# Transformer block on one core: queries projected transposed, with the two heads' halves sorted by transfers inside SBUF

## The reference

```python
mod = silu(c) @ wmod                      # per batch: sa, ca, ga, sb, cb, gb
h = layernorm(x) * (1 + ca) + sa
fused = h @ w_kv_a                        # q_c (192), kv_c (64), k_pe (64)
q = rmsnorm(q_c) @ w_qb                   # 16 heads of 128 (nope) + 64 (rotary)
kv = rmsnorm(kv_c) @ w_kvb                # per head: k_nope (128), v (128)
q_pe = q_pe * cos + rotate_half(q_pe) * sin     # and k_pe alike
scores = q_full . k_full / sqrt(192), causal softmax, @ v, @ w_o
x = x + ga * attention
h = layernorm(x) * (1 + cb) + sb
# 16 routed experts, top 4, at most 128 tokens each, and one shared expert
x = x + gb * (experts(h) + shared(h))
```

## Time and profile before

| what | value |
|---|---|
| median of 3 runs | 1230.08 us (1229.61 to 1230.75) |
| span of the profiled execution | 1228.7 us (its only own time on record) |
| TensorE / VectorE / ScalarE / POOL busy | 95% / 68% / 54% / 23% of the span |
| mean granted TensorE clock | 0.982 |
| first scores | 53.9 us |
| distance between pairs in mid-batch | 12.20 us |

### The profile page before, as it was taken

The page is one execution under the profiler, slowest core; times in us unless marked ns, Lnnn a source line. Parts: engine busy times, 40 slices in busy tenths (PEclk is TensorE's granted clock), DMA queues, the critical chain, the costliest instruction groups (busy, mean ns, idle before and its releaser), DMA issues.

```text
span 1228.7 us, 26041 instructions
## 1 busy us (share of the span) xinstructions
PE 1165.9 (95%) x7596; PEld 954.4 (78%) x7596; DVE 836.3 (68%) x2596; ACT 666.3 (54%) x1904; POOL 276.5 (23%) x332
## 2 busy tenths in 40 slices
PE   6799999999999999999999999999999999998792
PEld 3688878887788878887788779887788778886561
DVE  3577758776677668776777568776777668764541
ACT  2477635774477635774467626773467636672130
POOL 1000032221322132121312022211312122212364
PEclk8899999999999999999999999999999999999897
DMA  9520002000010001000010001000110001000793
GB/s 296 154 62 0 0 4 67 0 0 0 17 51 0 0 17 51 0 0 0 17 51 0 0 17 51 0 0 0 33 36 0 0 17 34 1 1 18 228 234 38
DMA packets 48157, 46.01 MB, mean 37 GB/s; under 512 B 10050, under 2 KB 44800, under 8 KB 48136
## 3 DMA queue, kind: packets, MB, share of 16 engines
q1 hardware_dynamic: 29096, 30.90, 8.5%
q0 software_dynamic: 7168, 6.20, 2.7%
q10 hardware_dynamic: 11872, 8.65, 2.5%
HBM read 35.04 MB, written 15.11 MB: 41 GB/s over the span
## 4 chain that ended last, share of the span: by engine, by line
PE 86%; DVE 4%; ACT 2%; POOL 2%; DMA 2%; SPq 1%; issue 1%; ACTq 1%; POOLq 0%; DVEq 0%
PE PS L691 11%; PE PS L712 11%; PE PS L830 8%; PE PS L670 7%; PE PS L671 6%; PE PS L672 6%; PE PS L656 4%; PE PS L838 4%; PE PS L859 3%; PE PS L643 3%; PE PS L646 3%; PE PS L647 3%; PE PS L644 2%; PE PS L645 2%; PE PS L809 2%; PE PS L701 2%
## 5 line engine op out<-in xcount | busy, mean ns | idle before, releaser
L1031 ACT ACTIVATE probs<-probs,nmax 128x512 f32<-128x512 f32 (+3 forms) x512 | 283.5, 555 | 167.6 <-DVE nmax L1275 164.1
L1275 DVE CUSTOM_DVE_ANT_0 probs<-PS,cmask 128x512 f32<-128x512 f32 (+3 forms) x512 | 230.4, 488 | 117.0 <-PE PS L672 114.7
L552 POOL DMA_INDIRECT tab_dram<-entry,slot x112 | 110.5, 987 | 386.7 <-PE PS L712 365.4
L670 PE MATMUL PS<-kTh,qTh 128*128 128x512 f32 (+3 forms) x512 | 174.5, 341 | 1.5 <-DVE qTl L1306 1.5
L672 PE MATMUL PS<-kTh,qTl 128*128 128x512 f32 (+3 forms) x512 | 164.9, 322 | 0.0
L671 PE MATMUL PS<-kTl,qTh 128*128 128x512 f32 (+3 forms) x512 | 164.9, 322 | 0.0
L691 PE MATMUL PS<-ident,probs 128*128 128x128 f32 x1280 | 164.8, 275 | 0.0
L1040 ACT ACTIVATE pT<-PS 128x384 f32<-128x384 f32 (+3 forms) x320 | 124.4, 461 | 68.0 <-PE PS L691 68.0
L712 PE MATMUL PS<-pT,kmat 128*64 128x512 f32 (+3 forms) x1024 | 151.9, 439 | 0.3 <-issue 0.3
L691 PEld LDWEIGHTS PS<-ident,probs 128*128 128x128 f32 x1280 | 141.4, 140 | 10.3 <-issue 7.4
L712 PEld LDWEIGHTS PS<-pT,kmat 128*64 128x64 f32 x1024 | 68.0, 136 | 76.0 <-issue 62.1
(11 more groups left out here) (256 smaller groups left out, 2084.8 us busy)
## 6 DMA issues: line engine op xcount, KB each, us to landing
x_in<-in_x SPq DMA_DIRECT2D x8, 512.0 KB, 6.0
modb<-mod_dram SPq DMA_DIRECT2D x8, 512.0 KB, 5.4
h_dram<-mod_dram SPq DMA_DIRECT2D x1, 4096.0 KB
h_dram<-h SPq DMA_DIRECT2D x8, 512.0 KB, 3.0
out<-base SPq DMA_DIRECT2D x8, 512.0 KB, 3.5
pT<-in_wo SPq DMA_DIRECT2D x1, 2048.0 KB, 11.0
tab_dram<-entry,slot POOLq DMA_INDIRECT x112, 2.1
oT<-in_wqnT SPq DMA_DIRECT2D x1, 1536.0 KB, 11.5
```

The source lines that it names most:

```text
L552: pool.indirect_dma_start(tab_dram[:, :], bass.IndirectOffsetOnAxis(ap=slot[:, j:j + 1], axis=0), entry[:, j, :], None, bounds_check=NE * ...
L670: pe.matmul(PS[:, bank, 0:n], qTh[:, h, rows_q], kTh[:, 0:n], start=True, stop=False)
L1031: act.activation(probs[:, UO[u]:UO[u] + UW[u]], probs[:, UO[u]:UO[u] + UW[u]], ACT.Exp, scale=-1.0, bias=nmax[:, u:u + 1], accum_out=psums ...
L1275: dve.tensor_tensor_reduce(out=probs[:, UO[u]:UO[u] + UW[u]], in0=PS[:, SBANK[u], 0:UW[u]], in1=cmask[:, S - UW[u]:S], scale=-1.0, scalar= ...
```

## The change

Queries are projected transposed: the weights (128 columns: latent or rotary numbers of both heads of a pair) are stationary and all 512 tokens move, so a pair's queries come out with features in rows, the latent ones in bank 6 and the rotary ones in bank 7. Rotation is done in this form, with tables by row: VectorE multiplies by cosine, and by sine for two 64-row halves crosswise; POOL adds, ScalarE makes the high part, POOL the low part. ScalarE and VectorE make the latent high and low part. All four lie in `qstage`, in which the rows are not sorted by heads; SP sorts them by six transfers inside SBUF into `qT` (two buffers), and the scores wait for these. This runs two pairs ahead instead of one. The pair loops are unrolled. In steps 6 and 7 outputs stand where the projections stood, and the h1 statistics and turns have moved to step 6.

```diff
+            def move(p, hl, lo, head, frm, n):
+                src = qstage[frm:frm + n, 2 * hl:2 * hl + 2, :].bitcast(F32)
+                sp.dma_start(qT[p % 2][lo:lo + n, :, head, :].bitcast(F32), src).then_inc(q_landed[p % 2], 16)
+            def move_query(b, p, fresh=False):
+                g = b * NPAIR + p
+                wait_alone(sp, latl_ready, g + 1)
+                if not fresh:
+                    wait_alone(sp, s_ps, NU * (g - 1))
+                for h in range(2):
+                    move(p, 0, 0, h, h * KL, KL)
+                wait_alone(sp, pel_ready, g + 1)
+                for h in range(2):
+                    for half in range(2):
+                        move(p, 1, KL + half * HALF, h, half * KL + h * HALF, HALF)
...
             sp.dma_start(h2_dram[0:T, H:].rearrange("(b s) h -> b s h", s=S),
                          mod_dram[:, 3 * H:].unsqueeze(1).to_broadcast([B, S, H])).then_inc(gates_out, 16)
+            for p in range(3):
+                move_query(0, p, p < 2)
             with sp.Fori(0, B - 1) as b:
                 n = b + 1
                 sp.wait_ge(h1_ready, n)
                 sp.wait_ge(res_ready, n)
                 sp.dma_start(x_in[:], rows(xr, n)).then_inc(x_landed, 16)
+                for p in range(3, NPAIR):
+                    move_query(b, p)
+                for p in range(2):
+                    move_query(n, p)
+                store_rows(b)
+                move_query(n, 2)
                 store_batch(b)
                 load_modb(n)
...
+            def query_rotary(g):
+                wait_alone(pool, turned_ready, g + 1)
+                pool.tensor_tensor(qr[:, 0, :], qr[:, 0, :], qr[:, 1, :], ALU.add).then_inc(rope_ready, 1)
+                wait_alone(pool, peh_ready, g + 1)
+                pool.tensor_tensor(qstage[:, 3, :], qr[:, 0, :], qstage[:, 2, :].bitcast(F32),
+                                   ALU.subtract).then_inc(pel_ready, 1)
...
+            with pool.Fori(0, B - 1) as b:
+                n = b + 1
+                roots_pre(n)
+                roots_post(b)
+                query_rotary(n * NPAIR)
+                rows_scaled(b)
+                query_rotary(n * NPAIR + 1)
+                rows_shifted(b, n)
+                counts(b, False)
+                query_rotary(n * NPAIR + 2)
+                shared(b)
+                for p in range(1, NPAIR - 1):
+                    if p + 2 < NPAIR:
+                        query_rotary(n * NPAIR + p + 2)
+                    scatter(b, p)
+                pool.wait_ge(scattered, n * NT * TOPK * 16)
                 pool.sem_inc(entries_free, 1)
...
-            def q_project(p, g, tiles):
-
-                cols = bass.ts(p, 2 * P)
...
+            def q_project(p, bank):
+
+                cols = bass.ts(2 * p + (bank == PEBANK), P)
+                pe.matmul(PS[:, bank, :], wq0h[:, cols], ql0h[:], start=True, stop=False)
...
+                    if u == 0:
+                        pe.wait_ge(q_landed[p % 2], landed(b, p))
...
+                last = p == NPAIR - 1
+                if p < NPAIR - 2:
+                    q_rotary(p + 2, g + 2)
+                elif not last:
+                    pe.wait_ge(turned_ready, (b + 1) * NPAIR)
                     pe.wait_ge(oT_ready, g)
-                    pe.wait_ge(qTl_ready, 2 * g + 2)
-                    output(1, 7, range(0, 3))
+                    output(1, PEBANK, range(0, 3))
                 else:
-                    q_project(p + 1, g + 1, (0, 1))
+                    if more:
+                        turn_h1(b + 1, 1, LATBANK)
+                    pe.wait_ge(oT_ready, g)
+                    output(1, PEBANK, (NPAIR - 3,))
...
+                scores(b, p, first, (3, 4))
+                if p < NPAIR - 2:
+                    q_latent(p + 2, g + 2)
+                elif not last:
+                    output(1, PEBANK, range(3, NPAIR - 3))
...
+                    output(0, LATBANK, range(0, 3))
+                scores(b, p, first, (5, 6, 7))
                 if not first:
                     values(g - 1, b)
...
                 turn_probs(g, first, (0, 1))
...
+                if last:
+                    output(0, LATBANK, range(3, NPAIR - 2))
                 turn_probs(g, first, (2, 3))
...
+                if p == NPAIR - 2 and more:
+                    pe.wait_ge(latl_ready, (b + 1) * NPAIR)
+                    turn_h1(b + 1, 0, LATBANK)
                 turn_probs(g, first, (4, 5))
                 spread_sums(g)
...
+                act.activation(qstage[:, 0, :], PS[:, LATBANK, :], ACT.Copy).then_inc(lath_ready, 1)
+
+            def rotary_high(b, p):
+                act.wait_ge(rope_ready, b * NPAIR + p + 1)
+                act.activation(qstage[:, 2, :], qr[:, 0, :], ACT.Copy).then_inc(peh_ready, 1)
...
                 maxima(g, (3, 4))
                 if first and more:
                     gated(b - 1, 0)
-                if last and more:
+                if p == NPAIR - 2 and more:
                     modulation(b + 1)
                     h1_statistics(b + 1)
+                for part in rope[:1]:
+                    part()
                 maxima(g, (5, 6, 7))
...
+                for part in rope[1:]:
+                    part()
+                if p == NPAIR - 2 and more:
                     h1_normed(b + 1)
                 invert_sums(g)
+                if rope and not first:
+                    q_low(g + 2)
```

More of the change, by code:

```diff
@@ L729, in step @@
                     shared_down(0)
-                scores(g, first, (3, 4))
-                if last:
-                    output(1, 7, range(3, NPAIR - 2))
-                else:
-                    q_project(p + 1, g + 1, (2, 3))
-                scores(g, first, (5, 6, 7))
+                scores(b, p, first, (3, 4))
[3 more added lines that the diff above has]
+                    output(1, PEBANK, range(3, NPAIR - 3))
+                else:
+                    if more:
+                        pe.wait_ge(hT_ready, 2 * (b + 2))
+                    else:
+                        pe.wait_ge(latl_ready, (b + 1) * NPAIR)
+                    output(0, LATBANK, range(0, 3))
+                scores(b, p, first, (5, 6, 7))
                 if not first:
@@ L924, in pairs @@
             def pairs(b, more):
-                with pe.Fori(1, NPAIR - 1) as p:
-                    step(p, b, False, False, more)
-                step(NPAIR - 1, b, False, True, more)
+                for p in range(1, NPAIR):
+                    step(p, b, False, more)
             pe.wait_ge(const_ready, 3)
@@ L1048, in sums_out, with step @@
                 act.activation(rb[:], PS[:, RBANK, :], ACT.Copy).then_inc(rb_ready, 1)
-            def step(p, b, last, more):
+            def step(p, b, more):
                 g = b * NPAIR + p
+                if p == NPAIR - 1 and more:
+                    turned_h1(b + 1, LATBANK, 1)
                 exps(g, (3, 4))
-                if not last:
-                    nope_copy(g + 1)
+                if 0 < p < NPAIR - 2:
+                    latent_high(b, p + 2)
                 exps(g, (5, 6, 7))
@@ L1057, in step @@
                 group_out(g, 1)
-                if not last:
-                    q_high(g + 1, 0)
-                    q_high(g + 1, 1)
-                elif more:
-                    turned_h1(b + 1, (6, 6))
+                if p == 0:
+                    latent_high(b, p + 2)
                 group_out(g, 2)
+                if p < NPAIR - 2:
+                    rotary_high(b, p + 2)
+                elif p == NPAIR - 2 and more:
+                    turned_h1(b + 1, LATBANK, 0)
                 group_out(g, 4)
                 sums_out(g)
-                if not last:
+                if p < NPAIR - 1:
                     exps(g + 1, (0, 1, 2))
             def pairs(b, more):
-                with act.Fori(1, NPAIR - 1) as p:
-                    step(p, b, False, more)
-                step(NPAIR - 1, b, True, more)
+                for p in range(1, NPAIR):
+                    step(p, b, more)
             def tanh_gate(b, k, m, bank):
@@ L1327, in step @@
                     gated(b - 1, 1)
-                if not last:
-                    q_low(g + 1, 0)
                 group_out(g, 3)
+                if rope and first:
+                    q_low(g + 2)
                 group_out(g, 5)
                 if not last:
-                    q_low(g + 1, 1)
                     maxima(g + 1, (0, 1, 2))
@@ L1521, in middle @@
                 if pre:
-                    for part in q_rope(n * NPAIR):
+                    for part in q_rope(n * NPAIR, not post):
                         part()
+                    q_low(n * NPAIR)
                 if not post:
```

292 lines of the change are left out of this document (150 added, 142 removed).

## The result

The changed kernel takes **1311.29 us** (median of 4 runs, 1310.08 to 1315.23), the kernel before 1230.21 us in the same session (1229.61 to 1230.75): ratio 1.0663, 95% interval 1.0634 to 1.0693. The forecast was 1236 with a range up to 1257: the sign is right, the size is not. The profiled execution has a span of 1309.1 us against 1228.7.

A forecast was written before the change was run, and what follows sets the result against it. TensorE was taken as the bound, without idle brackets in steady pairs. Minus 40.4, 6.0, 6.2, 1.4, 2.6 and 2.2, plus 38 and 27, gave plus 6 on 1230.1: 1236 us, range 1208 to 1257.

The forecast's parts named there:

- v+4.85, just in time: Steady pairs: VectorE's group 3 copy ends 4.85 us after the values start (v), so TensorE's next scores lose 0.
- unrolled loops: 0: Unrolled pair loops: no row shows a stall for instructions, so cost 0 (0 to 5).
- Steady pairs, minus 40.4: Steps 1 to 5 of eight batches: TensorE saves 1.01 us a pair, 40 x 1.01, with nobody else late.
- rival B: Steady pairs: POOL and VectorE shut each other out, scores wait 0.4 a pair, total 1254; chance 0.14.
- The middle, minus 1.4: Seven changes of batch: minus 0.2 each, with a wait of about 2 us before the h2 turns; bounds minus 7, plus 10.
- step 0 saves its turns: Middle: after first scores moved from 461.29 to 462.4, step 0 loses its query turns; part of minus 0.2 a batch.
- Step 6, minus 6.0, plus 38, minus 6.2: Step 6: less TensorE work, minus 6.0; h1 turns wait for POOL's root in six batches, plus 38; step 7, minus 6.2.
- Prologue, plus 27 minus 2.2: First queries queue behind the 4 MB gates spread, first scores at 79, plus 27; step 0 of batch 0 minus 2.2.
- Last batch's end, minus 2.6 and 1.1: Last batch: 12 outputs instead of 18 before the second residual, minus 2.6; its step 6 TensorE work, minus 1.1.
- A: Prologue: the queries' transfers pass the spread, removing a 25 us stall, total 1211; chance 0.14.
- C: Each pair: late transfers through the staging tile delay ScalarE's exponentials and TensorE, excess 0.8, total 1281; chance 0.05.
- D: Step 6: no stall, as POOL's last scatter comes earlier or VectorE is let past it, total 1198; chance 0.07.

The follow-up runs named there:

- run 4: Changed kernel with VectorE's steps 1 to 5 in a loop again, every other engine left unrolled: 1294.74 us, ratio 1.0532.
- run 6: Changed kernel with POOL's addition waiting until VectorE has copied (spread) the inverse sums: 1295.14 us, ratio 1.0521.
- run 8: Changed kernel with four repairs at once, those of run 1, run 4, run 6 and run 7: 1211.62 us, ratio 0.9843.
- run 9: run 8 without the repair of run 6, so POOL's addition and VectorE's copy meet again: 1240.31 us, ratio 1.0095.
- run 5: Kernel before the change with nothing but VectorE's steps 1 to 6 unrolled: 1268.07 us, ratio 1.0312.
- run 10: run 8 with the 4 MB spread of the gates issued by ScalarE before the last batch instead of in the prologue: 1219.93 us, ratio 0.9931.
- run 11: run 8 with the spread cut into eight 512 KB transfers, issued on ScalarE's queue at the start of each batch's middle: 1206.26 us, ratio 0.9794.
- run 1: Changed kernel with POOL's scatters in four steps of four instead of six steps of three with a last one: 1273.37 us, ratio 1.0347.
- run 2: Changed kernel with the 4 MB spread of the gates cut into eight transfers, one per batch, on SyncE's own queue: 1326.48 us, ratio 1.0778.
- run 7: Changed kernel with the whole 4 MB spread of the gates issued on ScalarE's queue in the prologue instead of SyncE's: 1295.96 us, ratio 1.0551.
- run 3: Changed kernel with one VectorE reciprocal writing all 512 columns, replacing a small reciprocal and the copy: 1423.99 us, ratio 1.1568.

## Why the prediction was wrong

Two steps failed above all: "v+4.85, just in time", which let VectorE's copy run undisturbed beside POOL's addition, and "unrolled loops: 0". Behind them come the middle and the work terms of the steps 6 and 7. No single one takes the result out of the range: without the stall at the jump it is still 1294.74 (run 4), without the exclusion 1295.14 (run 6).

**Steady pairs, minus 40.4: right on TensorE's work, wrong on who is late.** The work taken from TensorE is what was said: with the exclusion gone the 40 distances sum to 38.1 less (run 8; 449.8 against 487.9). In the changed kernel they sum to 10.0 less. The failing step is "v+4.85, just in time", a chain for VectorE that used 0.43 for the copy. I had the mechanism as rival B, with the right place (v+2.1, when POOL's addition starts) and a price of 0.4 a pair, 18 in all; it is 0.74 a pair, 28.7 in all (run 9; 27 to 31). It was priced low because "if it waits for that to end, group 3's copy ends at v+5.3" counts only a part: VectorE loses 1.0 and had 0.3 of room (1.0 less 0.74), not the 0.6 that its 0.4 left over. Giving it 0.14 with the argument "no row of before shows one waiting for the other" was the error of judgement: in the kernel before no addition of POOL's ran at one of the 64 copies. In 42 of them a scatter began, 0.2 to 0.4 behind the copy's start, and all 64 took 0.43. So the rows couldn't show it; that the two coincide in each pair was known.

**Unrolled loops, 0 (0 to 5): the term that was missing.** "No row shows a stall for instructions" was true and worthless, since the kernel before had the loop that prevents it. It cost 16.6 in the changed kernel (run 4) and 37 in the kernel before (run 5), and none of the rivals held it.

**The middle, minus 1.4 (minus 7 to plus 10).** Without the jump's stall the seven changes sum to 374.8 to 376.8, against 365.4: plus 9.3 to 11.4, at or just over the upper bound. The 2 us bracket before the h2 turns came as said, but not what it can do to the clock: in some changes the granted clock falls to 0.50 for 3.4 us behind it, which costs 1.7. This happens in the first change of the runs 8 and 10 (55.3 where the others take 53.6), in two of run 9 and in none of run 11. In the other changes of run 8 the first scores of a batch come 0.9 later than before, counted from the last values, and 1.1 was forecast. What failed is "step 0 saves its turns": from the first scores to the first values it takes 22.35, not less than before (21.85) but more. It has two further brackets, 0.30 for ScalarE's copy and 0.49 for VectorE's maxima, and from the end of its last projection to the values it takes 2.4 where before it took 1.3. Why VectorE and ScalarE are late there is open.

**Step 6, minus 6.0, plus 38, minus 6.2.** The stall is right in place, length and kind: 41.5 us in six batches (run 1), within 28 to 42; its clock part too (6.9 a batch, of which 4.9 are idle). Its work terms are too large: free of the stall, the stage is 3.3 shorter than before, not 12.2 (some 1.3 more lie in the last steady distance of each batch, which ends in step 6: 11.01 where the others take 11.17). In step 7 TensorE waits again, now for ScalarE's copy of the second h1 half: 0.73 before the outputs in run 8 (0.42 in the changed kernel). "Today's waits ... go with the statistics" overlooked that the turns themselves were moved close to their reader.

**Prologue, plus 27 minus 2.2.** Measured plus 25.0. The runs 2 and 7 split it: about 15 is the order in the queue, 3 what the spread costs beside the queries in another queue, and some 6 stay in every version (first scores 59.65 at best, 53.92 before): the transfers' own way, a bracket of 5.15, and a lower clock (0.77 from 60 to 70 us in run 2, 1.00 before). Between executions with the same prologue the first scores differ by up to 2.7 (53.92 and 51.23 in run 5), so the 3 is the least certain.

**Last batch's end, minus 2.6 and 1.1.** Measured minus 1.3 for the end, and minus 0.5 around its steps 6 to 8 (17.88 to 17.38): both too large.

**Rivals.** A (transfers pass the spread) is refuted by the 25.84 us bracket; B holds, by run 9, beside the forecast's own terms and not instead of them; C doesn't hold in the changed kernel's steady pairs, but is the next wait as soon as a transfer is put ahead (runs 2 and 10); D is refuted. The sum treated B as an alternative to the forecast, whereas each was free to be true with the others: 1236 + 29 + 17 is 1282, and the middle (10.7 over its term), the size of step 6's stall (3.5) and the work of step 6 and 7 (8.9) make up most of the 29 that are left.

## What to carry to other kernels

When a change moves an operation of POOL to where VectorE copies inside SBUF, price the meeting as a full wait for the first of the two, and look for a semaphore that makes POOL come second: here one wait was worth 27 to 31 us. Unrolling a loop inside a longer loop is not free on an engine that others wait for; leave it rolled on that engine, or measure the jump back. Repairs tried one at a time can hide each other: the same wait gained only 16 while the stall at the jump stood. An argument of the form "no row of before shows it" is worth nothing for a resource that the kernel before didn't use in that way. And a slower result may hide a sound idea: three repaired side effects and a loop turn plus 6.6% into minus 2.1%.

## What the runs showed of the hardware

- A VectorE reciprocal of 512 float32 columns takes 3.35 us (run 3), five times a product or a subtraction of the same size (0.68); one of 8 columns takes 0.20.
- A backward jump over a long body stopped VectorE for 3.5 to 5.2 us, and the six jumps went with 39 more packets on the instruction queue. In run 4, where the other engines' loops stay unrolled and the queue has 34 packets more than in the kernel before, ScalarE stands at its jumps too: 3.5 to 3.6 us idle, its next exponential 1.7 us behind the maximum that it waits for (0.4 in run 8). It is mostly hidden behind another wait.
- A copy of 512 columns inside SBUF that begins while a POOL addition (1.27 us) runs ends 0.28 to 0.29 us after it: 1.44 instead of 0.43 when it begins 0.12 after the addition, 0.85 when 0.70 after. With the addition second the copy takes 0.43.
- The granted clock fell to 0.50 for 3.4 us behind TensorE's idle stretch of 2.0 us in the middle in some changes of batch (the first of runs 8 and 10, two of run 9, the sixth of run 4) and stayed at 1.00 in the others; where it fell, the change took 1.6 to 1.7 longer.
- The same 4 MB transfer held up the first scores by 18.3 us when it was ahead of the queries in their queue, and by 3.0 when it was in another engine's (runs 2 and 7).
